# Forward substitution by 32-row blocks in place of doubling for the 128x128 triangular inverses of a delta-rule kernel

## The reference

```python
# z = layernorm(layernorm(x)); q, k, v = split(z @ gates_w + gates_b); lr = z @ lr_w + lr_b
k = k / norm(k)
K = tril(k @ k.T, -1)                       # 512 x 512
u = solve_triangular(K + eye, v, lower=True)
y = (q @ k.T) @ (lr * u) @ out_w + out_b    # every pair of tokens, no mask
# then a two-layer relu MLP with a layernorm, and a SiLU-gated feed-forward with quantised
# weights on layernorm(x); each part is added to its input
```

## Time and profile before

| | |
|---|---|
| median of 3 runs | 1593.3 us (1593.15 to 1595.68) |
| the profiled execution | 1594.8 us, its span 1593.1 us |
| busy PE, PEld | 99%, 88% |
| busy DVE, ACT, POOL | 72%, 50%, 49% |
| granted TensorE clock | 0.998 |

### The profile page before, as it was taken

How to read it: one execution, slowest core, us unless ns; L and a number is a source line. 1 busy time by engine, 2 the same in 40 slices (tenths; PEclk the granted TensorE clock), 3 DMA queues, 4 the chain that set the end, 5 groups by cost and what they waited for, 6 DMA issues and landing times.

```text
span 1593.1 us, 29859 instructions
## 1 busy us (share of the span) xinstructions
PE 1570.5 (99%) x10694; PEld 1403.0 (88%) x10694; DVE 1143.5 (72%) x2815; ACT 799.0 (50%) x1632; POOL 780.5 (49%) x918
## 2 busy tenths in 40 slices
PE   8999998899999999999999999999999999999998
PEld 8999997788888888888888888888888888888887
DVE  6767784577777677777776777777776666666664
ACT  6878774344444444444444444444444444444443
POOL 5446872244444454444444544444444444444442
PEclk9999999999999999999999999999999999999999
DMA  7999997112222322222223222222222222222200
GB/s 239 333 315 312 329 326 236 60 60 74 74 74 73 113 74 74 74 74 74 74 74 106 80 73 73 73 73 74 70 86 76 73 73 74 74 72 73 68 20 27
DMA packets 150164, 178.18 MB, mean 112 GB/s; under 512 B 78850, under 2 KB 132098, under 8 KB 141826
## 3 DMA queue, kind: packets, MB, share of 16 engines
q1 hardware_dynamic: 150018, 176.28, 33.7%
HBM read 98.64 MB, written 77.59 MB: 111 GB/s over the span
## 4 chain that ended last, share of the span: by engine, by line
PE 80%; DVE 2%; ACT 1%; POOL 0%; issue 0%; DVEq 0%; POOLq 0%; ACTq 0%
PE ps L174 33%; PE ps L1098 22%; PE ps L1108 11%; PE ps L1018 5%; PE ps L1029 4%; PE ps L1012 4%; PE ps L1139 0%; DVE z_lo L1462 0%; PE ps L246 0%; DVE low L198 0%; DVE low L218 0%; POOL work L1634 0%; DVE bs L1602 0%; ACT h_hi L1297 0%; DVE late L1487 0%
## 5 line engine op out<-in xcount | busy, mean ns | idle before, releaser
L1674 POOL TENSOR_TENSOR hl<-late,hh 128x512 fp32r<-128x512 f32 x128 | 165.4, 1292 | 206.4 <-ACT hh L1280 206.4
L1275 ACT ACTIVATE late<-ps 128x512 f32<-128x512 f32 x192 | 114.3, 595 | 170.6 <-PE ps L1098 170.5
L1108 PE MATMUL ps<-wdT,hh 128*128 128x256 f32 x744 | 198.1, 303 | 0.0
L1457 DVE TENSOR_TENSOR late<-ps,late 128x512 f32<-128x512 f32 x192 | 132.8, 691 | 87.0 <-PE ps L1098 85.1
L1284 ACT ACTIVATE z_hi<-ps 128x256 fp32r<-128x256 f32 x128 | 49.0, 382 | 288.1 <-PE ps L1029 288.1
L1108 PE MATMUL ps<-wdT,hl 128*128 128x256 f32 x744 | 181.7, 281 | 0.3 <-DVE hl L1462 0.3
L1280 ACT ACTIVATE hh<-late 128x512 fp32r<-128x512 f32 x192 | 120.8, 629 | 109.2 <-DVE late L1457 109.2
L1620 POOL TENSOR_TENSOR sc<-ls,mhalf 128x4 f32<-128x4 f32 x64 | 65.1, 1016 | 193.7 <-DVE ls L1424 193.7
L1656 POOL TENSOR_TENSOR xhm_lo<-xh,xhm_hi 128x1024 fp32r<-128x1024 f32 x32 | 76.4, 2387 | 164.3 <-DVE xhm_hi L1533 164.3
L1098 PE MATMUL ps<-xh3T_hi,wgT 128*128 128x512 f32 x384 | 153.7, 400 | 1.1 <-DVE xh3T_lo L1462 1.1
L1098 PE MATMUL ps<-xh3T_lo,wuT 128*128 128x512 f32 x384 | 152.1, 396 | 0.0
(11 more groups left out here) (217 smaller groups left out, 4776.4 us busy)
## 6 DMA issues: line engine op xcount, KB each, us to landing
xhT_scratch<-xhTk SPq DMA_DIRECT2D x32, 1024.0 KB, 6.7
xhT<-xhT_scratch SPq DMA_DIRECT2D x32, 1024.0 KB, 6.3
gg_scratch<-late SPq DMA_DIRECT2D x32, 640.0 KB, 4.2
gg<-gg_scratch SPq DMA_DIRECT2D x32, 640.0 KB, 3.9
xk<-in_L_attn_x_dram SPq DMA_DIRECT2D x32, 512.0 KB, 5.6
xt<-in_L_attn_x_dram SPq DMA_DIRECT2D x32, 512.0 KB, 4.0
out_dram<-late SPq DMA_DIRECT2D x31, 512.0 KB, 2.9
low_scratch<-late SPq DMA_DIRECT2D x128, 16.0 KB, 2.9
```

The costliest lines, as they stand in the source:

```text
L1108: mm = pe.matmul(ps[:, (FG, FU)[j // 2], (j % 2) * C:(j % 2 + 1) * C], part[:, h, blk(j)], wdT[:, h, :], start=(h == 0 and part is hh), st ...
L1275: act.activation(sg[:, h % 2, :], ps[:, FG, :], ACT.Silu, scale=QUANT).then_inc(sg_ev[h], 1)
L1457: dve.tensor_tensor(hf[:, h % 2, :], ps[:, up_bank(h), :], sg[:, h % 2, :], ALU.mult).then_inc(hf_ev[h], 1)
L1674: pool.tensor_tensor(hl[:, h, :], hf[:, h % 2, :], hh[:, h, :].bitcast(F32), ALU.subtract).then_inc(hl_ev[h], 1)
```

## The change

The three levels become a forward substitution by blocks of 32 rows: level 1 makes rows 32 to 63 of the inverse from its first 32 columns, level 2 rows 64 to 95 from its first 64, level 3 rows 96 to 127 from its first 96. Each has 32 weight columns and 32, 64 or 96 moving ones. The tile `x32` is renamed `xinv`; results are copied into it by VectorE, 32 partitions x 128, 256 and 384 elements (`below`, a plain copy in place of the addition), and it is the weights of the solve steps. `x64` and ScalarE's copy go. The load of the next `xinv` waits for the last solve step (`z_ps[0]`) in place of the third level. In `dve_body`, slot 4 of the inversion moves from before the output `dve_out(1)` and `dve_z(0)` to behind the two `dve_lo` of the MLP's transposed input, just ahead of slot 5.

```diff
-                    pe.matmul(ps[:, A1, 0:C], x64[:, j, :], wt[:, j, :], start=True, stop=True).then_inc(z_ps[j], 1)
+                    pe.matmul(ps[:, A1, 0:C], xinv[:, j, :], wt[:, j, :], start=True, stop=True).then_inc(z_ps[j], 1)
...
-                        pe_level(pe, A1, p_of, x32, 0, REST, slice(0, P), xa_ps)
+                        pe_level(pe, A1, p_of, xinv, 0, SUB, slice(SUB, HALF), xa_ps)
...
-                        pe_level(pe, A0, p_of, x64, 0, HALF, slice(HALF, P), xb_ps)
+                        pe_level(pe, A0, p_of, xinv, 0, HALF, slice(HALF, REST), xb_ps)
...
-                        pe_level(pe, A1, p_of, x64, 0, SUB, slice(REST, P), x128_ps)
+                        pe_level(pe, A1, p_of, xinv, 0, REST, slice(REST, P), x128_ps)
...
-                        wait(act, inv_in, i * 32 * QPB)
-                        after(act, z_ps[0], i)
-                        act.activation(x64[:, :, REST:P], x32[:, :, REST:P], ACT.Copy).then_inc(xd_tail, 1)
...
-                def plus(dve, bank, w, rows, src_ps, done, i):
+                def below(dve, bank, w, rows, src_ps, done, i):
                     dve.wait_ge(src_ps, i + 1)
-                    dve.tensor_tensor(x64[rows, :, 0:w], levels(bank, w, rows), x32[rows, :, 0:w], ALU.add).then_inc(done, 1)
+                    dve.tensor_copy(xinv[rows, :, 0:w], levels(bank, w, rows)).then_inc(done, 1)
...
-                        plus(dve, A1, REST, slice(0, P), xa_ps, xa_ev, i)
+                        below(dve, A1, SUB, slice(SUB, HALF), xa_ps, xa_ev, i)
...
-                        plus(dve, A0, HALF, slice(HALF, P), xb_ps, xb_ev, i)
+                        below(dve, A0, HALF, slice(HALF, REST), xb_ps, xb_ev, i)
...
-                        plus(dve, A1, SUB, slice(REST, P), x128_ps, x128_ev, i)
+                        below(dve, A1, REST, slice(REST, P), x128_ps, x128_ev, i)
...
-                    dve_invert(dve, m, r, 4, 5)
                     if down:
                         dve_out(dve, i, 1)
                     if att:
                         dve_z(dve, i, 0)
                     if mlp:
                         dve_lo(dve, x3l, x3h, (FO0, FO1), x3h_ev, x3l_ev, i)
-                    dve_invert(dve, m, r, 5, 6)
+                    dve_invert(dve, m, r, 4, 6)
...
-                    sp.wait_ge(x128_ev, n)
-                    sp.wait_ge(xd_tail, n)
-                    load_inv(sp, n, x32, inv_v)
+                    sp.wait_ge(z_ps[0], n)
+                    load_inv(sp, n, xinv, inv_v)
```

More of the change, by code:

```diff
@@ L130, in delta_block_kernel @@
         gg = sb("gg", [P, GW])
-        x32 = sb("x32", [P, TB, P])
+        xinv = sb("xinv", [P, TB, P])
         xT32 = sb("xT32", [P, TB, P])
@@ L312, in setup_pool @@
                 pool.memset(one4[:, :], 1.0)
-                pool.memset(x32[:, :, :], 0.0).then_inc(x32_zero, 1)
+                pool.memset(xinv[:, :, :], 0.0).then_inc(x32_zero, 1)
                 pool.memset(xT32[:, :, :], 0.0).then_inc(x32_zero, 1)
@@ L770, in load_first @@
                 sp.wait_ge(x32_zero, 2)
-                for t, v in ((x32, inv_v), (xT32, invT_v)):
+                for t, v in ((xinv, inv_v), (xT32, invT_v)):
                     for a in range(QPB):
@@ L923, in delta_block_kernel @@
             p1 = mb("p1", [P, TB, P])
-            x64 = mb("x64", [P, TB, P])
             HALF = P // 2
@@ L952, in delta_block_kernel @@
             rho_made = sems("rho_made", 3)
-            xd_tail, p1_zero, flipped = sem("xd_tail"), sem("p1_zero"), sem("flipped")
+            p1_zero, flipped = sem("p1_zero"), sem("flipped")
             pT_ps, pT_ev, xa_ps, xa_ev, xb_ps, xb_ev = (sem("pT_ps"), sem("pT_ev"), sem("x_a_ps"), sem("x_a_ev"),
@@ L1027, in pe_zstep @@
                         pe.wait_ge(x128_ev, i + 1)
-                        pe.wait_ge(xd_tail, i + 1)
-                    pe.matmul(ps[:, A1, 0:C], x64[:, j, :], wt[:, j, :], start=True, stop=True).then_inc(z_ps[j], 1)
+                    pe.matmul(ps[:, A1, 0:C], xinv[:, j, :], wt[:, j, :], start=True, stop=True).then_inc(z_ps[j], 1)
                 def pe_wstep(pe, i, j):
@@ L1319, in act_body @@
                         act_hh(act, i - 1, HB - 1)
-                    if att:
-                        wait(act, inv_in, i * 32 * QPB)
-                        after(act, z_ps[0], i)
-                        act.activation(x64[:, :, REST:P], x32[:, :, REST:P], ACT.Copy).then_inc(xd_tail, 1)
                     if mlp:
```

## The result

The changed kernel takes 1590.4 us, median of 18 runs (1588.1 to 1593.0), against 1593.3 of 18 runs of the kernel before (1592.1 to 1595.7): ratio 0.9982, 95% interval 0.9975 to 0.9989. That is inside the forecast range (1589.5 to 1597) and just short of the 0.2% that was named as the line to "faster", but the gain, 3.0 us, is almost four times the forecast 0.8. The profiled execution took 1588.4, its span 1586.7.

The account below looks back on a forecast made before the run. TensorE, 80% of the chain, was taken as the bound. Regular iterations -0.3, slot 4's copy -0.9, its ordinary steps +0.1, iteration 0 -0.1, iteration 1 +0.4: -0.8 us, median 1593.3 to 1592.5, range 1589.5 to 1597.

Parts of the forecast that it names:

- Level 1, -0.40: Level 1 on TensorE gets 0.49 us shorter, of which 0.40 is gained because the transposes then wait for GpSimd.
- The gate by GpSimd: The transposes' first load must wait for GpSimd's half of the MLP's input, following its end by 0.09 us.
- their own first load stands bare today too: At the transposes after level 1: their first load is already uncovered, so leaving narrow weights there costs nothing.
- Level 2, -0.03: Level 2 with 32 weight columns for 64: only the first load stands bare, saving 0.03 us, or 0 at the other end.
- Level 3, +0.42: Level 3 goes from 32 to 96 moving columns and costs 0.42 us more, between 0.40 and 0.49.
- The sum per regular iteration: The three levels nearly cancel: -0.01 us per regular iteration, from -0.12 to +0.09; -0.3 over 30 iterations.
- no wait for GpSimd: Low end per regular iteration, -0.12 us, if GpSimd doesn't hold the transposes; as a rival, chance 0.13, 1589.8 us.
- Switches: Narrow/wide weight changes on TensorE cost 0.10 us in, 0.11 out; level 1's new ones cost nothing, hidden by waits.
- The rival of a switch paid in full: Level 1's added weight-width switch costs 0.21 us in each of 31 iterations, giving 1599.0 us; chance 0.12.
- Copies, ScalarE, loads of `xinv`: VectorE's copies (0.30 to 0.55 us), ScalarE's dropped copy and the later `xinv` DMAs change nothing, all being covered.
- Slot 4, -0.9: Moving slot 4 cuts the stall in iterations 6, 14, 22 from 0.45 to 0.15 us: -0.3 each.
- The start: In the first two iterations: iteration 0 gains 0.1 us, iteration 1 loses 0.4 us.

Follow-up runs that it names:

- the two later sets: The changed kernel measured again twice, unaltered, beside the kernel before: ratios 0.9965 and 0.9977.
- the gate off: Changed kernel with GpSimd normalising one of its two tiles of the MLP's input, leaving work out, for timing only: ratio 0.9947.
- the wide level 3: Changed kernel with all 128 weight columns at level 3 instead of 32: ratios 0.9960 and 0.9970 to the kernel before.
- the slot-only kernel: Kernel before the change with slot 4 of the inversion moved and nothing else: ratio 0.9995.
- the kernel with all slots late: Changed kernel with 128 weight columns at level 3 and inversion slots 4 and 5 moved behind the first gate/up multiplication: ratio 0.9969.

## Why the prediction was right, and what of it was too small

"No difference, within the range" held, but narrowly and with some luck: the first set lies 0.9 us above the lower bound of 1589.5, and the ratios of the two later sets, applied to 1593.3, give 1587.7 and 1589.6, one below the bound and one on it. The bound itself was drawn in a little: the low ends in the prediction add up to -4.55 with the slot's and the start's terms, 1588.8. By its own steps:

- **Bound by TensorE's list: right.** Every regular iteration's gain is read off the distances of weight loads.
- **Level 1, -0.40: it was -0.44, and another -0.05 behind it.** The gate by GpSimd was real, but with 0.06 between its end and the load, not the 0.09 of iteration 1. And "their own first load stands bare today too" was wrong by 0.05: the transposes' group is that much shorter behind the narrow level 1 (its loads last 0.86 against 0.91 in the earlier trace rows). The pause at GpSimd's gate isn't what shortens it, since it is as short with the gate off; by what way the narrow group does isn't shown. Without the gate the two steps would have given 0.54 instead of 0.49.
- **Level 2, -0.03: -0.04. Level 3, +0.42: +0.41.** Both right; 96 moving columns with 32 of weights behave like the `xT32` product.
- **The sum per regular iteration is the step that failed in size.** Forecast -0.01, measured -0.13 (mean and median of the 24 iterations), at the end named for "no wait for GpSimd" (-0.12), which it reached another way: the wait was there. The error is in the term of level 1 (0.09) and in those of levels 2 and 3 (0.01 each). A difference of terms of 0.4 each was carried to a hundredth when its terms were off by up to 0.09; at -0.13, the 30 iterations of the forecast make 3.9 us, instead of 0.3.
- **Switches: right in the main.** Level 1's way in costs nothing that shows (its load stays at 2.01). On its way out the first two matmuls of the transposes stand 0.17 apart instead of 0.11, with the gate on and off; that 0.06 is inside the 0.49. The rival of a switch paid in full, 0.21, is out; the price of the two others is shown by the wide level 3.
- **Copies, ScalarE, loads of `xinv`: right,** nothing waits for them. The third copy has 0.56 against a bound of 0.55, and its cover is 0.48 against the 0.55 forecast.
- **Slot 4, -0.9: -0.7 to -0.8,** by the mechanism foretold, the wait being at `bt_lo` now. The copy itself took 1.25 there in iteration 14 instead of 1.09 (1.12 to 1.13 at the median). The ordinary steps cost nothing that the slot-only kernel shows.
- **Not foreseen: iterations 8 and 16,** -0.43 and -0.46, of which 0.13 each is the levels' and 0.6 in sum the vanished stall behind the scaling step. The prediction looked for waits that the new level 3 could bring, not for one that it could cover.
- **The start:** iteration 0 gained 0.19 in the profiled execution (forecast 0.1). Iteration 1 went from 44.33 to 44.84, but the executions of the same kernel differ from 44.38 to 45.03, and the slot-only kernel has 44.72; its +0.4 is neither shown nor refuted.

In the traces, iterations 2 to 30 take 5.2 us less: 24 x 0.13 = 3.2 for the regular ones, 1.15 for 6, 14 and 22, 0.9 for 8 and 16. The profiled spans differ by 6.4, since the part before the iterations differed by 1.6, a part that varies from 261.6 to 264.0 among the kernels here. The medians differ by 3.0, in the two later comparisons by 5.0 and 3.2. Part of that is the granted clock: at an equal one, 4.2 to 5.0 are measured. That the changed kernel has more runs at 0.996 is counted, but what makes the chip grant less there was not tried, and the 0.2 to 1.0 us between that and the traces' 5.2 stays open.

## What to carry to other kernels

On an engine that is always busy, cost matmul groups by the distance from load to load, separately for moving and weight columns: cutting 128 weight columns to 32 saved 0.48 us per iteration where 32 columns move, 0.11 where 64 do, and cost 0.09 where 96 do: the narrow group's load came together with its first matmul, the wide one's 0.24 ahead. When two large terms cancel, forecast their difference with the error of the terms times the number of iterations; and when a group gets short, look at the queues of the other engines between it and the place where the time is given back, since one of them may get the slack that takes a stall away.

## What the hardware showed that was not expected

VectorE's product of two SBUF operands, 0.40 us alone, took 1.51 when it started 0.05 after a GpSimd tensor_tensor of 1.29 us, and ended at 687.00, 0.27 after that one's end at 686.73. VectorE's operations that read PSUM beside the same GpSimd work keep their 0.68 or 0.69. In the kernel before the longest product of this kind took 1.19 us, in the changed one 1.71, both beside a longer GpSimd tensor_tensor that had started first, and both ended some 0.3 after it. Which of the two starts first matters: in iteration 12 of the kernel with all slots late VectorE's product (207 elements, at 767.18) and GpSimd's (767.17) started together, and VectorE's took its 0.38 while GpSimd's took 1.54 instead of 1.29. So where both engines read two SBUF inputs, one of them seems to wait for most of the other's time, and an inversion step is cheap or four times as dear depending on what GpSimd has begun. The spans on GpSimd are rough, and no run was made for this. The Trainium skill, VectorE: DVE Perf Modes, Two Vector instructions with no wait between them, mentions a second SBUF read interface shared with GpSimd; the rows fit it, though no run here separates the operands.
